# Eight DMA transposes on ScalarE's queue in place of 64 TensorE turns of the quantised x, with the order of four engines changed around them

## What is computed

```python
def fake_quant(x, scale, zp):
    q = jnp.clip(jnp.round(x / s + z), QMIN, QMAX)
    return (q - z) * s
x = x + tanh(g_xattn[0]) * matmul(fake_quant(layernorm(x)), fake_quant(ctx[:, :1024]...))
h = layernorm(x)
q = einsum('bi,ki->bk', h.mean(axis=1), Wq)
coeffs = softmax((q @ lora_keys.T) / sqrt(K))
x = x + tanh(g_ffn[0]) * (h @ W_org.T + sum_e coeffs[e] * (h @ lora_down[e]) @ lora_up[e])
# layer 1: x + attention(layernorm(x), ctx), then x + moe(layernorm(x))
```

## Time and profile before

| | value |
|---|---|
| median of 3 runs | 1279.76 us (1277.89 to 1282.87) |
| the profiled execution's own time | 1279.76 us |
| its span, first to last instruction | 1277.9 us |
| TensorE busy | 1241.7 us, 97% of the span |
| VectorE, ScalarE, GpSimd busy | 817.8, 487.6, 680.5 us |
| mean granted TensorE clock | 0.992 of full speed |

### The profile page before, as it was taken

The page is one execution under the profiler, slowest core; times in us unless marked ns, Lnnn a source line. Parts: engine busy times, 40 slices in busy tenths (PEclk is TensorE's granted clock), DMA queues, the critical chain, the costliest instruction groups (busy, mean ns, idle before and its releaser), DMA issues.

```text
span 1277.9 us, 17619 instructions
## 1 busy us (share of the span) xinstructions
PE 1241.7 (97%) x6696; PEld 532.0 (42%) x6696; DVE 817.8 (64%) x1433; ACT 487.6 (38%) x853; POOL 680.5 (53%) x300
## 2 busy tenths in 40 slices
PE   8997889999999999999999999999999999999998
PEld 6564444444444422222222222234554444444444
DVE  7877931233356678899989998626556855737632
ACT  3569321011111167777777777753163010010000
POOL 6004994800014378888889888981072653534510
PEclk9998989999999999999999999999999999999999
DMA  9464232300033235454545453431163342533301
GB/s 352 143 198 148 78 122 64 100 0 0 11 107 104 77 75 118 90 114 107 114 90 114 104 118 86 99 79 21 54 195 98 103 158 87 179 100 99 115 9 57
DMA packets 44523, 130.69 MB, mean 102 GB/s; under 512 B 6816, under 2 KB 17056, under 8 KB 40352
## 3 DMA queue, kind: packets, MB, share of 16 engines
q1 hardware_dynamic: 37392, 91.93, 22.3%
q0 software_dynamic: 4608, 33.56, 13.0%
q10 hardware_dynamic: 2448, 4.20, 0.9%
HBM read 85.49 MB, written 10.49 MB: 75 GB/s over the span
## 4 chain that ended last, share of the span: by engine, by line
PE 75%; DVE 12%; issue 2%; ACT 1%; DMA 1%; POOL 1%; SPq 0%; POOLq 0%; DVEq 0%; ACTq 0%
PE bank L625 45%; PE bank L880 9%; DVE mxp L1631 7%; PE bank L912 7%; PE bank L867 6%; PE bank L949 5%; DVE xn L1621 2%; PE bank L700 1%; PE bank L712 1%; DVE XTl L1518 1%; DVE X L1528 0%; POOL R L591 0%; DMA stage_pair<-wts_in 0%; DVE stats L1377 0%; ACT XTh L1127 0%
## 5 line engine op out<-in xcount | busy, mean ns | idle before, releaser
L1631 DVE TENSOR_REDUCE mxp<-bank 128x1 f32<-128x512 f32 x512 | 320.5, 680 | 60.8 <-PE bank L867 60.5
L1280 ACT ACTIVATE R<-bank 128x512 f32<-128x512 f32 x512 | 273.9, 601 | 116.1 <-PE bank L949 112.9
L625 PE MATMUL bank<-XTh,R 128*128 128x512 bf16 x896 | 278.5, 380 | 0.0
L591 POOL TENSOR_TENSOR R<-R 128x2048 f32<-128x2048 f32 x48 | 218.7, 4556 | 35.4 <-ACT R L1280 28.2
L625 PE MATMUL bank<-R 128*128 128x512 bf16 x960 | 209.2, 379 | 0.0
L625 PE MATMUL bank<-XTl,R 128*128 128x512 bf16 x448 | 170.4, 380 | 0.0
L613 POOL TENSOR_TENSOR R<-stage_pair,R 128x1024 bf16<-128x1024 f32 x32 | 75.0, 2359 | 144.9 <-DVE R L1780 86.5
L625 PEld LDWEIGHTS bank<-R 128*128 128x128 bf16 (+1 forms) x960 | 94.0, 98 | 113.2
L867 PE MATMUL bank<-R 96*128 96x512 bf16 x352 | 134.6, 383 | 4.9 <-DVE mxp L1631 3.0
L880 PE MATMUL bank<-R,stage_c 128*32 128x512 f32 x1024 | 137.2, 608 | 0.5 <-ACT R L1280 0.5
L949 PE MATMUL bank<-R 98*128 98x512 bf16 x352 | 134.2, 381 | 1.9 <-ACT R L1280 1.9
(11 more groups left out here) (194 smaller groups left out, 1530.0 us busy)
## 6 DMA issues: line engine op xcount, KB each, us to landing
stage_pair<-wts_in SPq DMA_DIRECT2D x35, 512.0 KB, 3.6
R<-R POOLq DMA_DIRECT2D x16, 1024.0 KB, 6.9
stage_pair<-R POOLq DMA_DIRECT2D x16, 1024.0 KB, 7.1
stage_pair<-w_in SPq DMA_DIRECT2D x32, 512.0 KB, 3.5
stage_c<-w_in SPq DMA_DIRECT2D x32, 512.0 KB, 3.6
R<-q_scr SPq DMA_DIRECT2D x48, 128.0 KB, 2.4
XTh<-ctx_t_in SPq DMA_DIRECT2D x11, 512.0 KB, 8.0
XTh<-ctx_nat_in SPq DMA_DIRECT2D x9, 512.0 KB, 4.5
```

The costliest lines, as they stand in the source:

```text
L591: pool.tensor_tensor(PS[(0, 1, 2, 1)[j]], PB[2 * j % 4], PB[2 * j % 4 + 1], ALU.add).then_inc(p_add, 1)
L625: mm = pe.matmul(o, a, m, start=first and a is ah and bs is bh, stop=last and a is al)
L1280: act.activation(PB[kt % 4][:, h * S:(h + 1) * S], bank[t_bank(g, t)][:, :], ACT.Exp, scale=float(HD) ** -0.5).then_inc(exp_done, 1)
L1631: dve.tensor_reduce(mxp[head // REP % 2][:, m, n // 2, n % 2:n % 2 + 1], bank[s_bank(u)][:, :], AX.X, ALU.max).then_inc(s_max, 1)
```

## The change

The eight tiles of quantised x are transposed by DMA from `XTl` into `R[2]` (`XQT`), issued by ScalarE (`turn_x`), one semaphore a tile. `R[2]` is free once keys and values are done (`kv_step`), and becomes the high part of `org` later, so GpSimd splits `up` ahead of `org` and `org` waits for the eight products (`nat_mm`). The two `column_sums` get banks of their own. Chunks 27 to 31, which VectorE did ahead of the first update, now stand between the first updates. `lora_hidden(1)` goes ahead of `lora_spread(0)`, in bank 0. VectorE waits for all eight transposes before update 2, whose `lo_parts` overwrites `XTl`.

```diff
-WT_LAYOUT = [("kv", 4), ("down", 4), ("org", 8), ("up", 4), ("q", 8), ("o", 8)]
+WT_LAYOUT = [("kv", 4), ("down", 4), ("up", 4), ("org", 8), ("q", 8), ("o", 8)]
-H_BANK = (7, 6, 7, 6, 1, 6, 7, 2)
+H_BANK = (7, 0, 6, 7, 1, 6, 7, 2)
+        XQT = R[2]
...
             keys_out(0)
             load_context(len(CHUNKS) - loaded[0])
-            load_weights(WT_AT["down"], 2)
+            keys_out(1)
+            load_weights(WT_AT["down"], 4)
             sp.wait_ge(c_done, len(CHUNKS))
             sp.dma_start(LQW[:, :], lora_q).then_inc(lqw_in, 16)
-            keys_out(1)
-            load_weights(WT_AT["down"] + 2, 2)
+            load_weights(WT_AT["up"], 4)
             load_weights(WT_AT["org"], 8)
-            load_weights(WT_AT["up"], 4)
...
             add_columns(0)
-            split_down(0)
-            split_down(1)
+            for i in range(4):
+                split_down(i)
             add_columns(1)
...
-            split_down(2)
-            split_down(3)
-            split_group("org", org_h, org_l)
             pool.wait_ge(k_out, 64)
             pool.wait_ge(x_pre, TT)
             split_group("up", up_h, up_l)
+            pool.wait_ge(nat_mm, TT)
+            split_group("org", org_h, org_l)
...
-                        mm = pe.matmul(bank[4 + h][:, :], onesb[:, :],
+                        mm = pe.matmul(bank[4 + 2 * b + h][:, :], onesb[:, :],
...
-                        mm = pe.matmul(pair(t)[h][:, :], XTh[:, k * D + t * P:k * D + (t + 1) * P],
+                        mm = pe.matmul(pair(t)[h][:, :], XQT[:, k * D + t * P:k * D + (t + 1) * P],
...
-            turn_quantised(0)
-            turn_quantised(1)
             pe.wait_ge(v_act, 4)
             column_sums(0)
-            turn_quantised(2)
             pe.wait_ge(k_lo, 8)
-            quantised_tile(0)
-            turn_quantised(3)
-            turn_quantised(4)
-            quantised_tile(1)
-            turn_quantised(5)
-            turn_quantised(6)
+            for t in range(3):
+                quantised_tile(t)
+            pe.wait_ge(cb_done, 2)
+            turn_behind(0, 0)
+            quantised_tile(3)
             pe.wait_ge(c_done, len(CHUNKS))
-            pe.wait_ge(cb_done, 2)
             column_sums(1)
-            turn_quantised(7)
-            quantised_tile(2)
-            pe.wait_ge(cb_done, 4)
-            turn_behind(0, 0)
-            for t in range(3, TT - 1):
+            turn_behind(1, 1)
+            for t in range(4, TT - 1):
                 quantised_tile(t)
                 turn_behind(t - 2, t % 2)
...
             lora_hidden(0)
+            pe.wait_ge(x_up, 2 * (TT - 1))
+            lora_hidden(1)
             lora_spread(0)
             turn_behind(TT - 2, 0)
             pe.wait_ge(cv_done, 2)
-            lora_hidden(1)
+            lora_hidden(2)
             turn_behind(TT - 1, 1)
...
+            def turn_x(t):
+                act.wait_ge(xq_done, t + 1)
+                act.wait_ge(kv_step, KT * B)
+                act.dma_start_transpose(out=per_tile(XQT)[:, :, t * P:(t + 1) * P],
+                                        in_=XQ[:, t * D:(t + 1) * D]).then_inc(xq_t[t], 16)
...
-            for i in range(TB):
-                chunks(24 + 2 * i, 26 + 2 * i)
-                if i == 1:
-                    kv_out(1)
-                add_rows(i)
+            for t in range(TB):
+                add_rows(t)
+            for t in range(2):
+                turn_x(t)
+            kv_out(1)
+            for t in range(2, TT):
+                turn_x(t)
+            chunks(24, 28)
...
-            for t in range(TT - 1):
-                quantised_out(t)
-                if t < TB:
-                    add_rows(TB + t)
             scale_rows(0)
-            quantised_out(TT - 1)
+            chunks(28, 31)
             scale_rows(1)
+            chunks(31, 32)
+            act.wait_ge(c_done, len(CHUNKS))
             for t in range(2, TT):
                 turned_out(t - 2)
                 scale_rows(t)
+                if t < 4:
+                    add_rows(2 * t)
+                    add_rows(2 * t + 1)
...
-            chunks(24, 28)
             kv_out(1)
-            chunks(28, 32)
-            gate_parts()
+            chunks(24, 27)
...
             quantised_update(0)
+            chunks(27, 30)
             quantised_update(1)
+            chunks(30, 32)
+            for t in range(TT):
+                dve.wait_ge(xq_t[t], 16)
+            quantised_update(2)
             column_terms(1)
-            dve.wait_ge(xq_turned, TT)
-            for t in range(2, TT - 1):
+            for t in range(3, TT - 1):
                 quantised_update(t)
```

More of the change, by code:

```diff
@@ L244, in build @@
         xq_done = sem("xq_done")
-        xq_turned = sem("xq_turned")
-        xq_t = sem("xq_t")
+        xq_t = [sem(f"xq_t{t}") for t in range(TT)]
         kv_step = sem("kv_step")
@@ L679, in column_sums @@
                     for k in range(KT):
-                        mm = pe.matmul(bank[4 + h][:, :], onesb[:, :],
+                        mm = pe.matmul(bank[4 + 2 * b + h][:, :], onesb[:, :],
                                        Q2[b][:, k * D + h * HALF:k * D + (h + 1) * HALF], start=k == 0, stop=k == KT - 1)
                 mm.then_inc(cs_mm, 1)
-            def turn_quantised(t):
-                if t >= 2:
-                    pe.wait_ge(xq_t, t - 1)
-                for k in range(KT):
-                    mm = pe.transpose(bank_b[6 + t % 2][:, k * P:(k + 1) * P], XQ[:, t * D + k * P:t * D + (k + 1) * P],
-                                      identb[:, :])
-                mm.then_inc(xq_turned, 1)
             def pair(m):
@@ L705, in quantised_tile @@
             def quantised_tile(t):
-                pe.wait_ge(xq_t, t + 1)
+                pe.wait_ge(xq_t[t], 16)
                 if t >= 2:
@@ L746, in _ @@
             pe.wait_ge(v_dve, 4)
[L747 to L748 removed]
             pe.wait_ge(v_act, 4)
             column_sums(0)
[L751 removed]
             pe.wait_ge(k_lo, 8)
[L753 to L758 removed]
+            for t in range(3):
[3 more added lines that the diff above has]
+            quantised_tile(3)
             pe.wait_ge(c_done, len(CHUNKS))
[L760 removed]
             column_sums(1)
[L762 to L766 removed]
+            turn_behind(1, 1)
+            for t in range(4, TT - 1):
                 quantised_tile(t)
                 turn_behind(t - 2, t % 2)
+            pe.wait_ge(cb_done, 4)
             pe.wait_ge(lqw_done, 1)
[L770 removed]
             lora_query(0)
@@ L773, in _ @@
             turn_behind(TT - 3, 1)
+            pe.wait_ge(const_in, 48)
             lora_scores(0)
-            pe.wait_ge(wt_done, WT_AT["org"])
+            pe.wait_ge(wt_done, WT_AT["up"])
             lora_hidden(0)
+            pe.wait_ge(x_up, 2 * (TT - 1))
+            lora_hidden(1)
             lora_spread(0)
@@ L779, in _ @@
             pe.wait_ge(cv_done, 2)
-            lora_hidden(1)
+            lora_hidden(2)
             turn_behind(TT - 1, 1)
             pe.wait_ge(h_lo, 1)
-            lora_hidden(2)
-            pe.wait_ge(h_lo, 2)
             lora_hidden(3)
             pe.wait_ge(x_up, 2 * TT)
+            pe.wait_ge(h_lo, 2)
             lora_query(1)
@@ L789, in _ @@
             lora_scores(1)
-            pe.wait_ge(h_lo, 4)
+            pe.wait_ge(h_lo, 3)
             lora_hidden(5)
             lora_spread(1)
+            pe.wait_ge(h_lo, 4)
             lora_hidden(6)
@@ L1510, in column_terms @@
                 for h in range(2):
-                    dve.tensor_scalar(CB[:, b, h * HALF:(h + 1) * HALF], bank[4 + h][:, :], qc[:, 3:4], None,
+                    dve.tensor_scalar(CB[:, b, h * HALF:(h + 1) * HALF], bank[4 + 2 * b + h][:, :], qc[:, 3:4], None,
                                       ALU.mult).then_inc(cb_done, 1)
@@ L1588, in _ @@
             lora_shares(1)
+            gate_parts()
             for u in range(JT, B * JT):
@@ L1870 @@
             chunks(a["L0_ffn_lora_down"].transpose(1, 0, 2).reshape(D, ER)),
+            chunks(a["L0_ffn_lora_up"].reshape(ER, D)),
             chunks(a["L0_ffn_W_org"].T),
-            chunks(a["L0_ffn_lora_up"].reshape(ER, D)),
             chunks(a["L1_xattn_Wq"]),
```

6 lines of the change are left out of this document (removed).

## The result

The changed kernel takes 1295.29 us, the median of four executions (1294.57 to 1296.98); the kernel before, run beside it, 1279.26 (1277.89 to 1282.87). The ratio is 1.0121, 95% interval 1.0108 to 1.0134: 15.5 us slower. The forecast was 10.0 us slower. The direction was called rightly and the time lies in the range, but the steps did not add up as written: steps 1 and 4 were wrong by some 6 and 10 us, in opposite directions.

The account below looks back on a forecast made before the run. It took the tiles' way round several engines, paced by VectorE, as the bound from 97 to 152 us, then TensorE. 4.2 + 8T - 6.2 with T = 1.52 gave +10.0 on 1279.76: 1289.8 us, range 1278 to 1302.

Parts of the forecast that it names:

- Step 1: ScalarE from 97.4 us: four row terms, two issues, values and keys, six issues; chunk 24 out at 105.8 + 8T.
- Step 4: VectorE's updates 0 to 3 with chunks 27 to 31 between: update 3 at 138.8 + 8T, against 137.07 before.
- T: Time one transposing DMA's issue holds ScalarE's queue: taken as 1.52 us, between 0.338 and 2.70.
- ScalarE's copies run on while the queue issues: Named sign that the forecast is wrong: ScalarE working on during the issues, which the sum counted as holding it up.
- Steps 2 and 3: VectorE's three chunks and column terms end at 111.1 + 8T; GpSimd adds 2.3 us, update 0 starts at 113.6 + 8T.
- Step 5: Late row terms on ScalarE make VectorE wait 0.5 and 1.9 us for low parts; TensorE reaches `lora_query(0)` 4.2 + 8T later.
- Step 6: `lora_hidden(1)` covers TensorE's 3.61 us stall and removes 2.6 us of low clock: 6.2 us given back.
- 8T - 2.1: The whole sum, 4.2 + 8T - 6.2 before rounding: +10.0 us with T = 1.52.
- Nearly plain issues: Rival: T between 0.34 and 1.06, so gain pays for loss; 1280.4 to 1286.2 us at most; chance 0.37.
- Late transfers: Rival: VectorE waits for the transposes to land before update 2; 1283.5 or 1311 us by landing time; chance 0.12.
- More gained: Rival: issues cost nothing and half of VectorE's 12 us idle waits vanish; time below 1273.4 us; chance 0.04.
- The low clock that might have cost up to 2.6 us at `lora_query(0)`: TensorE's pauses between 116 and 165 us may lower its clock: up to 2.6 us more; in the range, no own case.

Follow-up runs that it names:

- e3: Changed kernel with GpSimd's four `down` splits held until all 32 chunks are done: 1285.67 us, ratio 1.0064 to the kernel before.
- e6: Changed kernel with the row terms of tiles 4 to 7 added ahead of the first scaling: 1291.90 us, ratio 1.009 to the kernel before.
- e1: Kernel before with only the LoRA order changed, `lora_hidden(1)` in bank 0 ahead of `lora_spread(0)`: 1272.46 us, ratio 0.9952.
- e5: Changed kernel with transposes issued by SyncE and GpSimd's four `down` splits held until the last chunk: 1280.22 us, ratio 1.0001 to the kernel before.
- e9: Changed kernel with SyncE issuing transposes, all chunks before update 0, row terms after chunks and key/value copies, two `down` splits before second-batch additions: 1270.64 us, ratio 0.992.
- e2: Kernel before with four extra GpSimd additions, results unused, beside VectorE's chunks: 1283.75 us, ratio 1.0039.

## Why the prediction was right or wrong

**T.** Taken at 1.52 between 0.34 and 2.70, it is 1.30 (median issue). The value is 0.22 off, 1.8 us in the sum. The estimate of 1.35 from the Trainium skill's 32 cycles a tile (page "DMA: Bandwidth & Descriptors", section "Why a DMA increments its semaphore by 16 and not by 1") was nearer than the middle of the bounds; the trace's 1.30 agrees with it.

**Step 1 failed in its order, not in its mechanism.** It put 2T behind the four row terms. In the trace the first issue starts at 97.01, beside the first row term (96.94). Chunk 24 starts at 110.00, which is 110.6 on the time scale of the execution before; the step gives 105.8 + 12.2 - 1.1 = 116.9. Of the 6.3 us, 1.8 are T; the other 4.5 are the four issues that hide, two beside the row terms and two beside the copies of values and keys. The sign to look for had been named, "ScalarE's copies run on while the queue issues", and it showed, for the work ahead of the issues in the program. Work *behind* an issue does wait: 5.44 us ahead of chunk 24. (In the kernel before, chunks 24 to 27 all stood ahead of the copies of values and keys; the order shown for it begins behind the first two.)

**Steps 2 and 3 held.** Chunks 24 to 26 took 1.33 each, and update 0 started behind GpSimd's addition (2.51 us of waiting for it), at 119.19 and not 125.8.

**Step 4 failed.** It took 9.7 us from update 0 to update 1; the trace has 19.3. Chunks 27 to 29 were costed at 4.0 us, the price in a stretch where GpSimd is idle. They stand where GpSimd adds and splits and take 14.7. The wait of 1.1 that the step had there vanished inside them; the same happens at chunk 30's clip (2.17), so update 2 followed 8.6 us later where the step says 8.4. In all some 10 us were missing. This is the term that decided the size: e3 takes away 8.7 of it. The prediction had looked at GpSimd's queue only for what waits for it, never for what runs beside it. The rest of the step holds: with the splits gone (e3), update 0 to update 3 takes 26.1 us where the step has 25.2, and the one clip that stays long is 2.2 of it.

**Step 5 held.** The waits were 0.50 and 1.82; e6 takes 2.5 us from this stretch.

**Step 6 held**, 6.2 said and 6.4 measured (e1). Its 0.93 us for eight turns at full clock is half of a row that ran at the low clock; it fits only because those are other turns. The ones meant take 0.90 at full clock (140.53 to 141.43 in the trace before).

**Small sums.** Step 3 adds 2.3 to 111.1 and writes 113.6 for 113.4; the wait measured is 2.51. Step 1 begins its row terms at 97.4, for which no row is shown; on the time scale of the execution before they begin at 97.5.

**The sum.** Up to the mean the forecast has 4.2 + 12.2 = 16.4 us, and the table 20.2: 6 too much in steps 1 to 3, 10 too little in step 4. Less 6.4 leaves 13.8 at the query split. The profiled execution loses another 1.7 behind it, where the clock stays low longer behind the same 2 us wait (0.75 and 0.91 in the windows 470 to 480 and 480 to 490 us; before 0.83 in one window, 460 to 470). (The two profiled executions' own times are 14.8 us apart, not 15.5, because the event that the table counts from comes 0.6 us earlier in the changed kernel's.) The form 8T - 2.1 with the true T would have given 8.3. That the total lay nearer than its parts is luck: two errors cancelled in part.

**The rivals.** Nearly plain issues: no, 1.30 us is above the 1.06 from which the sum passes 0.5%; and e5 shows what the kernel is with neither cost, no change. What spoke for this rival was misread: not all issues in the trace before are under 0.6 us. GpSimd's take 0.87 (median of 32, none over 1.01), and single ones of SyncE up to 1.80. Late transfers: no, they land 3.4 us after the issue begins (median), and with twice as many still 3.3. More gained: no. The Trainium skill's "The three transpose paths" (page "VectorE: DVE Perf Modes") has 1309 ns for a block of 128x128, which as an estimate is 84 us for 64 blocks in series. The trace does not bear out that reading: the first issue begins at 97.0 and the last at 108.6 and lands some 3.4 us later, so 64 blocks take about 15 us. The low clock that might have cost up to 2.6 us at `lora_query(0)` cost nothing: TensorE paused (11.86 us once, ahead of tile 3) and ran a product of 16 matmuls in 5.46 us at 140.04, all of it under VectorE's chain; from update 3 to the mean only the two waits of step 5 are added.

**What stays open.** How long the clock stays low behind the 2 us wait 241 us after the query split differs between kernels (0 to about 3 us more), and no run changed that alone. It is part of what e9 loses behind the query split, and may be of the spread of e3's executions (mean granted clock 0.991 in the fastest, 0.988 in the slowest).

## What to carry to other kernels

Price an instruction by a row in which the same neighbours are at work. A VectorE `tensor_scalar` from SBUF to SBUF that costs 0.69 us alone costs up to 2.9 beside GpSimd, so moving VectorE's work into a gap is free only if GpSimd is idle there too; look at the engine beside, not only at the queues ahead and behind. A DMA that takes over a microsecond to issue belongs on a queue whose engine has nothing late behind it. And take a change apart before judging it: this one held a gain of 6.4 us, a cost that moves to another queue, and a collision, and the LoRA order alone beats the kernel before. Look for a price in the whole trace, too, not only in the stretch that changes: here a row at 22 us had it.

## What the runs showed of the hardware

- A transposing DMA of 128x1024 bf16, SBUF to SBUF, holds its queue 1.30 us (median, after; longest 3.04) on ScalarE and 1.28 (e9; longest 3.61) on SyncE, against 0.338 for a plain one on ScalarE. It lands mostly 3.2 to 3.4 us after its issue begins, at most 6.3 (e9).
- ScalarE's queue runs ahead of ScalarE: two issues went out beside four activations that stand ahead of them in the program. What stands behind the issues waits.
- VectorE's `tensor_scalar` from SBUF to SBUF, 1024 columns, waits for the whole GpSimd instruction under way (0.69 to 2.86 us; 0.29 to 1.85 for 8 columns), and GpSimd's next one loses 0.3 to 0.45 us; one in e2 got through. On one column it is not touched (0.15 to 0.27), nor are VectorE's statistics (0.68) and its `scalar_tensor_tensor` with one input in PSUM (1.40 for two).
